# A dynamic 1x1 convolution behind a group norm: last chunk by tiles, GpSimd normalises two chunks, scale operations and idle matmuls

## What is computed

```python
xn = group_norm(x, 32 groups)                       # _gn
pooled = mean(xn over pixels)
h = relu(batch_norm(pooled @ fc_w.T))               # 32 hidden values
ch_att, fl_att = sigmoid(h @ ch_w.T + ch_b), sigmoid(h @ fl_w.T + fl_b)
kn_att = softmax(h @ kn_w.T + kn_b)                 # over 4 kernels
agg_w = einsum('bk,koc->boc', kn_att, weight)       # one 512x512 matrix per sample
y = einsum('bchw,boc->bohw', xn * ch_att, agg_w) * fl_att
out = x + batch_norm(y)
```

## Time and profile before

| | us |
|---|---|
| median of three runs | 2103.95 |
| lowest, highest | 2103.34, 2104.27 |
| the profiled execution: its span | 2101.4 |
| TensorE busy in it | 2054.3 (98%) |
| VectorE busy | 1898.9 (90%) |
| ScalarE busy | 1726.0 (82%) |
| GpSimd busy | 12.8 (1%) |

### The profile page before, as it was taken

The page is one execution under the profiler, slowest core; times in us unless marked ns, Lnnn a source line. Parts: engine busy times, 40 slices in busy tenths (PEclk is TensorE's granted clock), DMA queues, the critical chain, the costliest instruction groups (busy, mean ns, idle before and its releaser), DMA issues.

```text
span 2101.4 us, 33109 instructions
## 1 busy us (share of the span) xinstructions
PE 2054.3 (98%) x10848; PEld 1061.1 (50%) x10848; DVE 1898.9 (90%) x3065; ACT 1726.0 (82%) x2307; POOL 12.8 (1%) x25
## 2 busy tenths in 40 slices
PE   3979999999999999999999999999999999999999
PEld 2535555555555555555555555555555555555554
DVE  8879999999999999999999999999999999999974
ACT  5858888888888888888888888888888888888885
POOL 0100000000000000000000000000000000000000
PEclk9999999999999999999999999999999999999999
DMA  9976656565556565556655566655565655566522
GB/s 334 224 217 207 207 189 206 204 210 199 195 199 206 196 210 196 205 193 209 208 195 203 188 205 207 210 196 194 200 206 199 210 194 204 195 208 207 180 105 106
DMA packets 239644, 421.60 MB, mean 201 GB/s; under 512 B 7552, under 2 KB 236928, under 8 KB 239616
## 3 DMA queue, kind: packets, MB, share of 16 engines
q1 hardware_dynamic: 237888, 415.74, 58.3%
q0 software_dynamic: 1728, 5.51, 1.4%
HBM read 210.19 MB, written 205.52 MB: 198 GB/s over the span
## 4 chain that ended last, share of the span: by engine, by line
PE 93%; DMA 5%; DVE 1%; ACT 1%; SPq 0%; issue 0%; POOL 0%; DVEq 0%; POOLq 0%
PE product L854 31%; PE product L856 31%; PE product L855 31%; DMA out<-x_ring 3%; DMA x_ring<-x 1%; DMA x_ring<-y 1%; PE small L821 0%; SPq L216 0%; DVE chunk_stats L441 0%; ACT w_hi L344 0%; ACT x_norm L262 0%; DVE mixed_weight L625 0%; ACT x_hi L328 0%; DVE x_ring L455 0%; ACT x_hi L271 0%
## 5 line engine op out<-in xcount | busy, mean ns | idle before, releaser
L854 PE MATMUL product<-x_hi,w_hi 128*128 128x448 f16 x3552 | 1253.2, 353 | 11.7 <-DVE x_lo L449 10.3
L855 PE MATMUL product<-x_lo,w_hi 128*128 128x448 f16 x3552 | 1253.1, 353 | 0.0
L856 PE MATMUL product<-x_hi,w_lo 128*128 128x448 f16 x3552 | 1253.0, 353 | 0.0
L283 ACT ACTIVATE y<-product,out_bias,out_scale 128x448 f32<-128x448 f32 x892 | 638.7, 716 | 262.3 <-PE product L856 259.0
L262 ACT ACTIVATE x_norm<-x_ring,norm_bias,norm_scale 128x448 f32<-128x448 f32 x892 | 668.2, 750 | 0.0
L455 DVE TENSOR_TENSOR x_ring<-x_ring,y 128x896 f32<-128x896 f32 x434 | 465.4, 1084 | 80.3 <-ACT y L283 76.0
L854 PEld LDWEIGHTS product<-x_hi,w_hi 128*128 128x128 f16 x3552 | 350.3, 99 | 337.8 <-DVE x_lo L449 11.2
L441 DVE BATCH_NORM_STATS2 chunk_stats<-x_ring 128x6 f32<-128x448 f32 x896 | 492.2, 612 | 22.6 <-DMA x_ring<-x 20.4
L856 PEld LDWEIGHTS product<-x_hi,w_lo 128*128 128x128 f16 x3552 | 347.8, 98 | 324.1 <-issue 1.3
L855 PEld LDWEIGHTS product<-x_lo,w_hi 128*128 128x128 f16 x3552 | 347.8, 98 | 321.1 <-issue 2.9
L449 DVE TENSOR_TENSOR x_lo<-x_norm,x_hi 128x1792 f16<-128x1792 f32 x222 | 447.6, 2016 | 14.9 <-ACT x_hi L271 14.9
(11 more groups left out here) (93 smaller groups left out, 327.8 us busy)
## 6 DMA issues: line engine op xcount, KB each, us to landing
x_ring<-x SPq DMA_DIRECT2D x224, 896.0 KB, 4.8
out<-x_ring SPq DMA_DIRECT2D x223, 896.0 KB, 3.9
x_ring<-y POOLq DMA_DIRECT2D x12, 448.0 KB, 7.5
weight<-wt SPq DMA_DIRECT2D x8, 512.0 KB, 12.9
out<-x_ring SPq DMA_DIRECT2D x4, 224.0 KB, 1.9
params<-par SPq DMA_DIRECT2D x1, 462.0 KB, 12.1
```

What stands on the lines that cost most here:

```text
L283: nc.scalar.activation(y[:, s % 2, t], acc[k % BANKS][:, 0:COLS], ACT.Identity, bias=obias[:, t:t + 1], scale=oscale[:, u, t:t + 1]).then_ ...
L854: nc.tensor.matmul(bank, whi[:, u, t, cols], hi, start=(t == 0), stop=False)
L855: nc.tensor.matmul(bank, whi[:, u, t, cols], lo, start=False, stop=False)
L856: ins = nc.tensor.matmul(bank, wlo[:, u, t, cols], hi, start=False, stop=(t == CT - 1))
```

## The change

Four things, all in the first turn:

1. SP loads chunk 6 of sample 0 by four DMAs, one per channel tile, and VectorE's statistics wait per tile.
2. The weight scale: `weight_unscale` and the rescaling step go; catt follows the reciprocal at once; bn_scale and out_scale are made later, behind `first_split(1)`, with a semaphore (`oscale_ready`) that ScalarE waits for ahead of its first evacuation.
3. GpSimd normalises chunk 1 and then chunk 0 to fp32, eight operations of 128x448, in place of VectorE's `first_norm` (4) and ScalarE's `norm(start, 1, t)` (4). The four of chunk 0 write y and wait until the absolute-value passes are done with it.
4. `keep_awake`: 32 instead of 22, four new ones between the two transfers of the top, ten instead of six behind them.

```diff
-                load(slot // CHUNKS, slot)
+                if slot == CHUNKS - 1:
+                    cols = slice(slot * COLS, (slot + 1) * COLS)
+                    for t in range(CT):
+                        landed = tile_in[t] if t < CT - 1 else chunk_in[slot]
+                        sp.dma_start(xs[:, slot, t], x_d[0, :, t, cols]).then_inc(landed, 16)
+                else:
+                    load(slot // CHUNKS, slot)
...
             mix_first(3)
             weight_hi(2)
-            norm(start, 1, 0, True)
-            norm(start, 1, 1, True)
             weight_hi(3)
-            norm(start, 1, 2, True)
-            norm(start, 1, 3, True)
             for t in range(CT):
                 norm(start, 2, t, True)
             split(start, 2)
+
+            act.wait_ge(oscale_ready, 1)
...
-            def stats(turn, f, t):
-                if t == 0:
+            def stats(turn, f, t, alone=False):
+                if alone and t < CT - 1:
+                    dve.wait_ge(tile_in[t], 16)
+                elif alone or t == 0:
...
-                return nc.vector.tensor_scalar(catt[:, :], sig[:, 0:CT], wscale[:, 0:1], None, ALU.mult)
+                return nc.vector.tensor_scalar(catt[:, :], sig[:, 0:CT], wscale[:, 0:1], W_TOP, ALU.mult, ALU.mult)
...
             step(nc.vector.reciprocal(wscale[:, :], wall[:, :]))
-            step(nc.vector.tensor_scalar(unscale[:, :], wall[:, :], 1.0 / (W_TOP * X_SCALE), None, ALU.mult))
             after(start)
-            step(nc.vector.tensor_scalar(wscale[:, :], wscale[:, :], W_TOP, None, ALU.mult))
-            step(nc.vector.tensor_scalar(inv[:, :], inv[:, :], unscale[:, 0:1], None, ALU.mult))
-            scaled_attentions(start, 0).then_inc(catt_ready, 1)
+            nc.vector.tensor_scalar(catt[:, :], sig[:, 0:CT], wscale[:, 0:1], W_TOP, ALU.mult,
+                                    ALU.mult).then_inc(catt_ready, 1)
...
             first_split(1)
+            step(nc.vector.tensor_scalar(inv[:, :], inv[:, :], wall[:, 0:1], 1.0 / (W_TOP * X_SCALE), ALU.mult, ALU.mult))
+            after(start)
+            nc.vector.tensor_tensor(oscale[:, 0], sig[:, CT:2 * CT], inv[:, :], ALU.mult).then_inc(oscale_ready, 1)
...
             add_kernel(3, 3)
-            first_norm(0)
-            first_norm(1)
             first_split(3)
-            first_norm(2)
-            first_norm(3)
-            dve.wait_ge(xn0_ready, CT)
+            dve.wait_ge(first_xn_ready, 2 * CT)
...
+            pool.wait_ge(norm_ready, 1)
+            for s in (1, 0):
+                for t in range(CT):
+                    if s == 0 and t == 0:
+                        pool.wait_ge(abs_done, 2 * KERNELS)
+                    nc.gpsimd.tensor_scalar(xn0[:, t] if s == 0 else xn[:, 1, t], xs[:, s, t],
+                                            nscale[:, 0, t:t + 1], nbias[:, 0, t:t + 1],
+                                            ALU.mult, ALU.add).then_inc(first_xn_ready, 1)
...
-            keep_awake(22)
+            keep_awake(32)
             pe.wait_ge(wsum_ready, 1)
             nc.tensor.matmul(top_row, wsum1[:, 0:1], p_("ident"), start=True, stop=True).then_inc(top_moved, 1)
+            keep_awake(4)
             pe.wait_ge(wtop_ready, 1)
             nc.tensor.matmul(top_all, ones[0:1, :], wtop[0:1, 0:1], start=True, stop=True).then_inc(top_moved, 1)
-            keep_awake(6)
+            keep_awake(10)
```

More of the change, by code:

```diff
@@ L135, in build @@
         wscale = sb("weight_scale", [P, 1])
-        unscale = sb("weight_unscale", [P, 1])
         acc = [ctx.enter_context(nc.psum_tensor(f"product_{k}", [P, 512], f32)) for k in range(BANKS)]
@@ L157, in build @@
         chunk_out = [sem(f"chunk_out_{k}") for k in range(RING)]
+        tile_in = [sem(f"tile_in_{t}") for t in range(CT - 1)]
         order = sem("vector_order")
@@ L164, in build @@
         wtop_ready = sem("wtop_ready")
+        oscale_ready = sem("oscale_ready")
         const_ready = sem("const_ready")
@@ L193, in build @@
         bn_ready = sem("bn_ready")
-        xn0_ready = sem("xn0_ready")
+        first_xn_ready = sem("first_xn_ready")
         first_hi_ready = sem("first_hi_ready")
@@ L352, in _ @@
             act.sem_inc(mix0_ready, 1)
-            act.sem_inc(xn_ready, 1)
+            act.sem_inc(xn_ready, 2)
             act.sem_inc(hi_ready, 2)
@@ L603, in _ @@
                 for t in range(CT):
-                    stats(start, f, t)
+                    stats(start, f, t, f == CHUNKS - 1)
             stats_complete(start, 0)
@@ L640, in first_split @@
                                                    op0=ALU.mult, op1=ALU.subtract).then_inc(first_w_ready, 1)
-            def first_norm(t):
-                nc.vector.tensor_scalar(xn0[:, t], xs[:, 0, t], nscale[:, 0, t:t + 1], nbias[:, 0, t:t + 1],
-                                        ALU.mult, ALU.add).then_inc(xn0_ready, 1)
             dve.wait_ge(att_ready, 1)
@@ L688, in _ @@
             dve.wait_ge(first_hi_ready, 2 * CT)
-            dve.wait_ge(xn_ready, 2)
             nc.vector.tensor_tensor(xlo[:, 1], xn[:, 1], xhi[:, 1], ALU.subtract).then_inc(lo_ready, 1)
```

## The result

| | before | after |
|---|---|---|
| median of the timed runs, us | 2103.66 (2103.34 to 2104.27) | 2172.2 (2170.63 to 2174.59) |
| span of the profiled execution, us | 2101.4 | 2169.1 |
| VectorE's idle "issue" ahead of chunk_stats, us | not among its waits | 58.3, in 26 pieces |
| TensorE's idle time for x_lo, us | 10.3 (2 times) | 56.0 (15 times) |
| TensorE busy, us | 2054.3 | 2076.2 |

A forecast was written before the change was run, and what follows sets the result against it. Bound: the moment TensorE is released for good, near 154 us, set by ScalarE's first evacuations. Gains 0.19 + 0.31 - 0.08 + 1.33 = 1.75 us off 2103.95 gave 2102.2 us (55%), range 2101.0 to 2106.6.

The forecast's parts named there:

- Nothing the change does can be won or lost: From 160 to 1600 us TensorE is always busy, so only the moment that stretch begins could matter.
- every rival: VectorE and GpSimd in each other's way (25%), TensorE late (10%), GpSimd too slow (4%), body not rigid (6%).
- Last chunk by tiles: Opening loads: per-tile loading lets the last chunk's VectorE statistics start at most 0.19 us earlier.
- Scale operations: Behind the reciprocal at 35.50: fewer operations bring w_hi(0) 0.31 us; with the tiles, w_hi(3) comes 0.42 earlier.
- Two normalisations off ScalarE's path: Between w_hi(3) and the first evacuation, two normalisations of 0.66 us leave ScalarE: 1.33 us gained.
- under a microsecond to spare: TensorE's low parts of the first two tiles, done at 50.9, stay ahead of evacuations at 51.16 and 51.8.
- GpSimd's price: Opening: each of eight GpSimd normalisations takes 1.0 us (bounds 0.47 and 3.5), all hidden.
- Matmuls on ones: TensorE before the weight sum and after: added matmuls are hidden and worth nothing to the evacuations.
- Rigid body up to 154 us: Everything behind the first evacuations shifts with them, until TensorE's last wait near 154 us; 1.75 us earlier.
- the first rival: VectorE's attention chain and weight adds: GpSimd operations hold VectorE back, 4.0 us in the mean, 2106.2 us; 25% chance.
- The 2.55 us from span to time: The timed median's excess over the profiled span before the change, carried over unchanged to the forecast time.

The follow-up runs named there:

- pad7: The changed kernel plus seven do-nothing increments at the start of VectorE's program, so its loop stands as before the change: 2103.25 us against 2102.67.
- no_gpsimd: The changed kernel with the eight normalisations back on VectorE and ScalarE, plus two padding increments on VectorE: 2103.12 us against 2102.44 before.
- gaps: The changed kernel with GpSimd normalising chunk 1 only, in two pairs, chunk 0 back on VectorE, plus three padding increments: 2101.08 us against 2102.44 before.
- before_pad79: The kernel before the change with 79 do-nothing increments at the start of VectorE's program: 2153.2 us, 77 instruction packets.

## Why the prediction was wrong, step by step

**"Nothing the change does can be won or lost" from 160 us on: the step that failed.** It was read off a trace in which TensorE is never idle there, and it took the loop's own cost per turn as fixed. What changed is where the loop lies. Of all that the change moves I counted operations, waits and transfers, and not the code behind them, though six operations and a wait less ahead of VectorE's loop could be counted in the diff. In its place the runs show a loop that is fetched again in each of 13 turns: 58.3 us of VectorE's idle time, 45.7 us more of TensorE's behind it, and 68.5 us in all, which seven instructions of padding give back. That is forty times the sum that I worked out, and lies outside of every rival. The trace of before could have given one warning: 12 instruction packets on q14 and 16 on q8 in a run of 33109 instructions mean that loops are held, and what is held can be lost. It did not tell how near the edge was (4 instructions).

**Last chunk by tiles: 0.19 predicted.** The last eight statistics of after run without a pause:

```profile
17.63 4.31 DVE L448 BATCH_NORM_STATS2 chunk_stats<-x_ring 128x6 f32<-128x448 f32 x8 [0.22 <-DMA x_ring<-x]
```

Against the earlier trace rows the pause of 0.19 is gone as predicted; the chunk before the last itself came 0.27 earlier, which no step foresaw, and in pad7 0.18 (17.72).

**Scale operations: 0.31 and, at w_hi(3), 0.42.** By no_gpsimd, where GpSimd doesn't disturb, w_hi(0) starts at 36.07 instead of 36.41, 0.34 for both parts together where I had 0.50, and w_hi(3) at 45.89 instead of 46.08, 0.19 where I had 0.42. The matmuls on ones took part of it: VectorE idles 0.37 us ahead of 34.56, for the first transfer of the top, which TensorE makes behind the 32.

**Two normalisations off ScalarE's path: 1.33.** From w_hi(3) to the first evacuation were 6.83 us (46.08 to 52.91), in after 5.52 (47.10 to 52.62). The term holds, 1.31. But w_hi(3) itself came 1.02 later instead of 0.42 earlier, in the main by the 1.6 us on VectorE. Together: 52.62, 0.29 earlier than before, where 51.16 was predicted. In gaps, without that loss, it is 51.84, and there 0.24 of waiting for TensorE's low parts shows: the "under a microsecond to spare" was spent.

**GpSimd's price: 1.0 predicted, 0.70 and 1.07 measured,** done at 38.3, hidden. The slope of the earlier trace rows was a fair guide.

**Matmuls on ones: worth nothing, as predicted,** but their time is no fixed number: 32 take

```profile
27.97 5.15 PE L839 MATMUL product<-ones 128*128 128x256 f16 x32
```

in after, 6.08 in no_gpsimd and 6.52 in pad7. In after they are about 0.21 us apart up to 31 us and 0.11 behind it; in pad7 the change comes near 34. (The clock column of the windows reads 1.00 from 28 us on in both, so there it is the spacing that shows the change.) What sets its moment is left open: the two kernels differ by the seven increments alone. From 37.4 to 50 us after has the full clock (1.00, before 0.84), and TensorE spends it waiting for w_lo: 10.36 us busy there instead of 12.54.

**Rigid body up to 154 us.** TensorE's last wait of the opening ends at 154.07 before, at 154.01 in after, 154.00 in pad7, 153.47 in no_gpsimd and 150.83 in gaps, with first evacuations at 52.91, 52.62, 52.77, 52.71 and 51.84. 0.29, 0.14 and 0.20 us at the start came with 0.06, 0.07 and 0.60 there; 1.07 us became 3.24 once. The body is rigid only roughly, and whether that larger step is bought by the earlier start or is play between executions stays open, since the timed medians of gaps and before are not told apart.

**Two smaller things in the sums.** From 0.45 us per GpSimd operation on, the first rival was to decide; no sum gives that number, and the forecast's gain is used up at 1.75 / 8 = 0.22. The 2.55 us from span to time set the median of three runs against one other execution; where both are known of the same execution, they are 1.8 apart (2170.93 and 2169.1 in after, 2103.57 and 2101.8 in pad7).

Had the loop stayed in place, the forecast's sum would have been about 1.5 us too good and its verdict, no difference, right: pad7 is that kernel.

## What to carry to other kernels

A loop's place in the code is part of every edit ahead of it, on its own engine: count the instructions that an edit takes out or puts in ahead of a loop, and if the time changes evenly in a stretch whose work is the same, look at the number of instruction packets and for idle "issue" at the top of each turn before any other theory. Padding by a few instructions that do nothing settles it in one run, and repairs it. GpSimd work that is hidden by itself can still lengthen VectorE operations beside it, with two inputs and with one: compare durations of the same operation, not gaps.

## What the runs showed of the hardware that was not expected

- VectorE's instructions came in packets of 8 KB. A loop of 302 instructions ran without being fetched again as long as it lay within 384 of them that begin at a boundary (d from 0 to 82), and was fetched in each turn, five packets, when it began 1 to 3 instructions ahead of it or ended 1 or 22 behind.
- A jump back to what has to be fetched left VectorE idle for 2.7 to 3.8 us, a boundary met right behind it for 1.6 to 2.3 more, and 5.6 when the two fell together. The cost in the whole is 30 to 88 us (1.4% to 4.2%) for 13 turns.
- After 3.48 us of idling, ahead of 457.16, TensorE of after resumed at full clock, fell to 1.2 GHz within a microsecond, and was back at 2.4 GHz (1.00) in the window from 462 us. The length of the idle time alone doesn't decide: in before, 3.40 us ahead of 118.19 were followed by a granted clock of 1.00 from 118 to 126 us, and in before_pad79 2.58 us ahead of 323.41 by one of 0.67 from 324 to 328.
- A 128x448 fp32 normalisation on GpSimd took 0.70 us, and 1.07 in the mean beside VectorE's weight adds. Beside one, a small VectorE operation with one tensor input took 0.57 us in place of 0.17.
